# One output projection of each batch moved to the fourth n of its own batch, and no residual addition while GpSimd adds exponentials

## The reference

```
kqv = layernorm(x) @ Wqkv + bqkv
q, k, v = kqv[:, :, 0], kqv[:, :, 1], kqv[:, :, 2]
scores = jnp.einsum('bsnh,btnh->bnst', k, q) / math.sqrt(HEAD_SIZE)
scores = jnp.triu(scores) + -10000.0 * jnp.tril(ones, k=-1)
attn = jax.nn.softmax(scores, axis=2)
out = jnp.einsum('bnkq,bknh->bqnh', attn, v)
x = x + layernorm(out.reshape(b, s, 512) @ Wo + bo)
h = silu(g) * u        # g, u: layernorm(x) times dequantised gate_w, up_w
x = x + layernorm(h @ Wd)
```

## Time and profile before

| | us |
|---|---|
| median of 3 runs | 1638.31 |
| lowest, highest | 1636.98, 1640.26 |
| the profiled execution | 1638.2 |
| its span, first to last instruction | 1636.3 |

### The profile page before, as it was taken

The page is one execution under the profiler, slowest core; times in us unless marked ns, Lnnn a source line. Parts: engine busy times, 40 slices in busy tenths (PEclk is TensorE's granted clock), DMA queues, the critical chain, the costliest instruction groups (busy, mean ns, idle before and its releaser), DMA issues.

```text
span 1636.3 us, 24454 instructions
## 1 busy us (share of the span) xinstructions
PE 1543.4 (94%) x9286; PEld 642.0 (39%) x9288; DVE 948.3 (58%) x1897; ACT 796.6 (49%) x1284; POOL 596.5 (36%) x812
## 2 busy tenths in 40 slices
PE   4899999999999999999998999999999999999997
PEld 2333333333433333343332344444444444444443
DVE  5657766689666878667876333554434343434344
ACT  5356666567666666755786743232222222222222
POOL 4335664677665667746765310020000000000001
PEclk9899999999999999999999999999999999999999
DMA  4221322114421233222355431221111111111000
GB/s 180 91 53 42 83 59 53 53 62 108 122 45 28 85 98 96 73 53 50 107 168 157 129 102 40 58 97 39 45 27 52 26 52 26 52 26 52 0 26 26
DMA packets 113398, 112.26 MB, mean 69 GB/s; under 512 B 69632, under 2 KB 69632, under 8 KB 113024
## 3 DMA queue, kind: packets, MB, share of 16 engines
q1 hardware_dynamic: 113280, 110.69, 24.0%
HBM read 45.37 MB, written 25.17 MB: 43 GB/s over the span
## 4 chain that ended last, share of the span: by engine, by line
PE 72%; POOL 14%; DVE 5%; issue 5%; ACT 3%; POOLq 0%; ACTq 0%; DVEq 0%
PE ps L968 27%; PE ps L889 15%; PE ps L985 13%; PE ps L952 10%; POOL pt L1459 7%; PE ps L926 4%; DVE mcol L1247 2%; POOL rs L1379 1%; PE ps L902 1%; POOL pt L1450 1%; POOL stage L1443 1%; POOL atl L1469 1%; PE ps L910 1%; POOL rs L1376 1%; ACT tq L1074 1%
## 5 line engine op out<-in xcount | busy, mean ns | idle before, releaser
L1101 ACT ACTIVATE pt<-ps,nrm 128x512 f32<-128x512 f32 (+1 forms) x640 | 360.7, 645 | 220.6 <-PE ps L926 202.7
L968 PE MATMUL ps<-x2in,gu 128*128 128x512 f16 x2048 | 462.4, 379 | 0.0
L1247 DVE TENSOR_REDUCE mcol<-ps 128x1 f32<-128x512 f32 (+2 forms) x600 | 305.7, 575 | 149.9 <-PE ps L910 76.6
L968 PEld LDWEIGHTS ps<-x2in,gu 128*128 128x128 f16 x2048 | 200.2, 98 | 241.9 <-ACT sg L1122 0.5
L1376 POOL TENSOR_SCALAR rs<-mv 128x1 f32<-128x1 f32 x120 | 29.9, 249 | 644.7 <-DVE mv L1146 638.2
L1318 DVE SCALAR_TENSOR_TENSOR hf<-ps,usc,sg 128x512 f32<-128x512 f32 x128 | 96.1, 751 | 259.3 <-PE ps L968 245.7
L1127 ACT ACTIVATE hh<-hf 128x512 f16<-128x512 f32 x128 | 80.7, 630 | 258.1 <-DVE hf L1318 244.5
L1459 POOL TENSOR_TENSOR pt<-pt 128x1024 f32<-128x1024 f32 x84 | 203.4, 2442 | 1.8 <-ACT pt L1101 1.8
L952 PE MATMUL ps<-pt,v 128*32 128x512 f32 (+3 forms) x1536 | 189.2, 506 | 1.8 <-DVE rec L1279 1.7
L985 PE MATMUL ps<-wd,hh 128*128 128x512 f16 x496 | 188.0, 379 | 0.0
L985 PE MATMUL ps<-wd,hl 128*128 128x512 f16 x496 | 188.0, 379 | 0.0
(11 more groups left out here) (125 smaller groups left out, 1590.1 us busy)
## 6 DMA issues: line engine op xcount, KB each, us to landing
qpack<-stage SPq DMA_DIRECT2D x192, 64.0 KB, 2.0
kpack<-stage SPq DMA_DIRECT2D x192, 64.0 KB, 2.0
xr<-in_x SPq DMA_DIRECT2D x32, 256.0 KB, 2.8
x1d<-xr SPq DMA_DIRECT2D x32, 256.0 KB, 2.1
x2d<-xh SPq DMA_DIRECT2D x32, 256.0 KB, 2.0
x1in<-x1d SPq DMA_DIRECT2D x8, 1024.0 KB, 6.1
out_x<-yy SPq DMA_DIRECT2D x32, 256.0 KB, 2.0
xin<-in_x SPq DMA_DIRECT2D x24, 256.0 KB, 2.9
```

Of the source, the lines that this page charges most:

```text
L968: mm = pe.matmul(bk, GU[:, c, m, i * 128:(i + 1) * 128], x2in[:, 1 - k, p, c, :], start=p == 0 and c == 0, stop=p == 1 and c == 3)
L1101: act.activation(Pt[:, PBUF[step], h, off:512], ps[:, BANK[job], off:512], ACT.Exp, scale=esc).then_inc(s_ex, 1)
L1247: mm = dve.tensor_reduce(mcol[:, n % 2, col:col + 1], scores, AX.X, ALU.max)
```

## The change

It edits `projections` and the rule for `residual` in `row_work`. The third output projection of a batch (t = 8b + 2) moves from the first n of the next batch to s9 of the fourth n of its own; the later ones move up one place each, and one leaves the second n (its s8 stands without a projection now). One "vproj" goes from the fourth n to the third, which has nine projections instead of eight, in s4 and s6 but no longer in s5. In the fourth n, s5 has the first "woproj" in place of a "qk", and "qk" takes s2. The last batch's n = 15 is as it was. `residual` is put in no step s5 to s7 of the first 14 n.

```diff
     if n + 2 < NG:
-        for i, s in enumerate(((0, 2, 3, 7) if b else (1, 3, 7, 9), (0, 1, 2, 3), (1, 3, 7, 9), (1, 3, 5, 8))[g]):
+        for i, s in enumerate(((0, 2, 3, 7) if b else (1, 3, 7, 9), (0, 1, 2, 3), (1, 3, 7, 9), (1, 2, 3, 8))[g]):
             out[s] = ("qk", n + 2, i % 2, i // 2)
...
     if b + 1 < B:
-        first = 8 * b + 8 + (0, 0, 2, 6)[g]
-        for i, s in enumerate(((), (7, 9), (0, 2, 5, 8), (0, 2))[g]):
+        first = 8 * b + 8 + (0, 0, 2, 7)[g]
+        for i, s in enumerate(((), (7, 9), (0, 2, 4, 6, 8), (0,))[g]):
             out[s] = ("vproj", first + i)
     if g == 3:
-        for i, s in enumerate((5, 7, 9) if n == NG - 1 else (7, 9)):
+        for i, s in enumerate((5, 7, 9)):
             out[s] = ("woproj", 8 * b + i)
     elif b > 0 and g < 2:
-        for i, s in enumerate(((1, 5, 8, 9), (5, 8))[g]):
-            out[s] = ("woproj", 8 * b - 8 + (2, 6)[g] + i)
+        for i, s in enumerate(((1, 5, 8, 9), (5,))[g]):
+            out[s] = ("woproj", 8 * b - 8 + (3, 7)[g] + i)
     return out
...
+def adding(step):
+    return step < NS * SUMS and 5 <= step % NS <= 7
...
+            if kind == "residual" and adding(step):
+                continue
```

## The result

| kernel | median us | lowest, highest | ratio to before (95% interval) |
|---|---|---|---|
| before, beside the changed one | 1636.98 | 1631.17, 1640.26 | |
| changed | 1642.48 | 1639.88, 1645.24 | 1.0037 (1.0023 to 1.0050) |

Slower by 0.37%, 5.5 us between the medians, where 16 us less were forecast. The profiled execution of the changed kernel took 1639.89 us (span 1638.1), so the profile shows 1.8 us of loss in the span and not the whole 5.5. What follows is therefore told as lengths of n and of steps, from the first exponential of one to that of the next, and not as times since the start.

What follows compares the result with a forecast made beforehand. PE sets the pace nearly everywhere, GpSimd some of the end. Terms 3.6 + 5.0 + 2.8 + 4.0 - 0.9 + 1.5 = 16.0 us off 1638.2 give 1622; range 1611 to 1634.

Steps and rivals of the forecast that it cites:

- the sentence on SP's queue: SP's loads and stores move with their jobs by a step or two; costed at nothing.
- The fourth n: n = 3, 7, 11: GpSimd earlier, PE's mask wait in s7 goes; 1.2 each, 3.6 us gained.
- The first n: n = 4, 8, 12: shorter waits for mask and `norm`, less added masking on PE; 5.0 us gained.
- the 0.5 us for s5 to s7: First n: the residual leaves GpSimd's additions, taking 0.5 us off the 2.26 us mask wait.
- The second n: n = 5, 9: 3.0 + 1.0 + 0.9 - 3.5 = 1.4 each, 2.8 us gained.
- 3.0 for s6 and s7 together: Second n: residual gone from s5, additions shorter, one chain fewer; 3.0 us gained, bounds 1.0 and 5.4.
- rival (a): Turns in s5 to s7 replace the residual, holding DVE; 1630, chance 0.20. Sign: turns over 2 us, PE awaiting maxima.
- The price in s2: s2 of n = 5 and 9: three chains ahead of the mask; PE waits, lower clock, 3.5 us lost.
- The third n: n = 6, 10: s2 gains 2.9, extra projection loses 0.9; 2.0 each, 4.0 us gained.
- n = 2: No output projection to gain from, only the extra projection: 0.9 us lost.
- n = 14: Less DVE work ahead of it, where PE waits for DVE's maxima: 0.5 us gained, 1.5 with n = 13.
- (d): Slower: row-work chains ahead of masks in s0 and s2 delay GpSimd, 3.5 us a place; 1643, chance 0.11.

Runs made afterwards that it cites:

- experiment 1: Changed kernel with the load of tile 21 issued on SP ahead of the 24 copies: 1631.06 us, ratio 0.9965.
- experiment 10: The six pieces, with first-normalisation turns kept out of s6 and s7 of n = 1, 5 and 9: 1629.07 us, ratio 0.9949.
- the table alone: Changed kernel without its rule for `residual`, projections placed as in the changed kernel: 1630.94 us, ratio 0.9961.
- The six pieces: Changed kernel, the 24 copies per n issued four at a time behind s0 to s5 of the next n, not in one block: 1627.69 us, again 1627.06.
- 2: Changed kernel with the loads of tiles 5, 13 and 21 issued ahead of the copies: 1632.04 us, ratio 0.9975.
- 9: Experiment 1 with GpSimd's third small chain behind the masks in s2 of n = 5 and 9: 1632.98 us, ratio 0.9966.
- experiment 11: The six pieces, with first-normalisation turns kept out of s6 and s7 of n = 1 alone: 1627.61 us, ratio 0.9937.

## Why the prediction was wrong

**The step that failed** is the sentence on SP's queue, "I cost them at nothing", with its reason: "none of PE's waits in the earlier trace rows is for a DMA". That is true of the rows and no argument, since the change moves residuals against their loads. Nor do the loads all "move with their jobs by a step or two": the load of 21 stayed, and its residual came three steps earlier. What had to be counted is in the list of jobs: where the load of each moved residual is issued, and what stands on SP between that and the residual. `packs` was named nowhere in my working. The runs put 11 us on it (1642.5 to 1631.1 with one DMA moved, 1637.0 to 1647.9 with one moved the other way). The sentence's last half, that a turn's copy may wait for its buffer, happened too, at 3.19 us in experiment 1, from the same block.

**The fourth n**: -3.5 us against -3.6. PE's wait of 1.41 us at the mask of s7 is gone. Right.

**The first n**: -5.0 against -5.0. Right in size, but not by its parts alone: the 0.5 us for s5 to s7 is too small for what the rule does there. Without the rule n = 4 is 56.33 and not 54.64, with PE idle 2.35 us in s7 instead of 1.66 and one stretch at the lower clock. The forecast did not see that the table without the rule would lose that clock. By steps of n = 4 against before, s1 gained 1.36 us (1.2 forecast) and s3 1.55 (0.8, for s3 and s4); s5 to s8 gained nothing, since s7 gained 0.26 and s8 lost 0.55; and s0 and s2 lost 0.9. That these come to 5.0 in three n is in part luck.

**The second n**: -1.8 against -2.8. s6 is 4.02 us as was said (4 to 5), but s7 went from 6.23 to 9.88. I took 3.0 for s6 and s7 together, and they gave 1.7; the turn at 400.68 took 2.61 us, the sign of rival (a), but experiment 10 shows that what bounds s7 of n = 5 is GpSimd. The stretch at the lower clock was halved (6.8 us to 3.4), not removed. The price in s2 was taken at 3.5, a wait and a lower clock; the wait came with 2.00, the clock stayed up, and s2 lost 2.0. s1 and s8 gained 1.28 and 0.96, near 0.9 and 1.0; s0 and s3 lost 0.7 and 0.4, which the sum did not have.

**The third n**: -0.1 against -4.0. Its s2 gained 3.0 in n = 6 (2.9 forecast). Then s3 lost 3.2. The forecast had written that two `norm` and two turns come into s3 and that "the projection in s4 hides most". The size was off because of residual 7 in s2, queued behind a tile of x that SP had issued late; without SP's lateness s3 is 6.68 instead of 8.20, so 1.5 us of the 3.2 are the queue's again. Of the other 1.7, the table alone has 0.5 (5.46 against 4.97 before), and 1.2 came with the row work that the rule moved in.

**n = 2**: +1.03 against +0.9. **n = 14**: three us more, of which s0 has 0.6, with DVE's row maxima late, and 3.2 are two steps at the lower clock. The kernel before had one stretch of it there, its variants one or two, the table alone one, all others two. The half microsecond forecast did not come. No run isolates this.

**The sum without the stall.** The six pieces are the changed order without the late loads. Against before their profile has +1.0 us in n = 2, -3.6 in the fourth n, -5.0 in the first, -2.1 in the second, -2.1 in the third, +0.6 in n = 13 and 14, +1.4 in n = 15 and 0.1 elsewhere: -9.7, and the medians -10.3. Forecast were -16. So of the 20.5 us by which the forecast missed the changed kernel some 15 are SP's queue (1642.5 to 1627.4), and the other 5 to 6 are terms of the wrong size: 0.7 in the second n, 1.9 in the third, 2.1 in n = 13 and 14, and 1.4 in n = 15, a stretch at the lower clock in its s2, whose scores, products and projections stand as before.

**The rivals.** (d) gave the right side and nearly the right time, 1643, by the wrong mechanism, so by luck: the chains stand ahead of the masks, and only s2 of n = 5 and 9 feels them. No rival had SP's row in it. (a)'s long turns came: the turn of 2.61 us in s6 of n = 5, with PE's wait of 1.67 for the maxima behind it, is the very sign that the forecast had named for being wrong. In n = 5 they cost nothing by themselves (experiment 10); where they did cost, in n = 1, they stood before the change as well. The table alone ran at 1631, near (a)'s 1630, for other reasons.

## What to carry to other kernels

When a job moves, follow its DMAs on the issuing queue as a list of their own: for each one, what must be issued ahead of it and how long that takes. A queue whose mean load is low can still hold a block of many small copies, and a load that stands behind it arrives by the block's length later, however short the load. Cut such a block up and put the pieces where their own deadline is far, above all before making rules for other engines tighter. And ask of each wait that an experiment shortens which engine needs the moved piece next; here the edits of 2, 9 and 10 (in n = 5) each took a visible wait away, and the wait of another engine stood beside it or right behind it.

## What was not expected of the hardware

- A copy of 64 KB between two places in SBUF took 0.62 us of SP's time to issue (4.96 us for eight) in most groups, and 0.77 in some (6.13), while a load of 256 KB of x from HBM took 0.34 to 0.53 in the timeline of the changed kernel around n = 13. In these rows the issue time does not go by the bytes.
- The wait of 9.6 us is followed by 8.7 us of work at a mean clock of 0.64, although PE had been at the upper level until it stopped at 820.25; the lower one was granted from 822.4 to 836.1. The stall costs 12.4 us in its step, 9.0 of them in longer idle time and 3.4 in the slower clock after it.
- A stretch of 3.4 us at the lower level costs 1.6 us where PE is what all wait for (n = 6 in the first experiment, 58.71 against 57.09), and 0.15 where PE waits for GpSimd anyway (s7 of n = 9: 9.88 against 9.74 us, with 3.4 us of it and none).
- Where such a stretch falls does not hang on the order of the instructions near it alone. n = 9 has the same order in the six pieces and in experiment 11 and took 58.38 and 60.12 us. In the changed kernel, the same order but for SP's, it took 58.55 in one profile and 60.11 in the other. So a difference of 1.6 us in one n between two profiles can be the place of such a stretch and not the edit. Two kernels were profiled twice: the spans of the six pieces differ by 2.9 us, 2.7 of it in the start of n = 0, and those of the changed kernel by 2.3 us, with 2.1 in that start, 1.6 more in n = 9 and 0.8 less in n = 13. What decides the place stays open.
